# A third tile of state 7 accumulated by VectorE in step 8, and the last image's membrane added by VectorE

## What is computed

```python
def step(h, t):                      # layer 0, over the pixels; 16 states n
    dA = jnp.exp(dt_t[:, :, None] * A)
    dB = dtN_t * B_t
    h = dA * h + dB[:, None, :] * x_t[:, :, None]
    y = jnp.einsum('bdn,bn->bd', h, C_t) + Dskip * x_t
...
def step(v, x_t):                    # layer 1, over the images
    v = v + (x_t - (v - V_RESET)) / TAU
    s = atan_spike(v - V_THRESHOLD)
    v = V_RESET * s_d + v * (1.0 - s_d)
...
x = x + _L0_conv_ref(_gn(x), ...)
x = x + _L1_conv_ref(_gn(x), ...)
```

## Time and profile before

| | |
|---|---|
| median of 3 runs | 4340.82 us (4330.65 to 4343.32) |
| the profiled execution | 4342.65 us |
| its span, first to last instruction | 4340.7 us |
| busy: VectorE, GpSimd, PE, ScalarE | 91%, 89%, 83%, 80% |
| time in the 768 pairs of scans on VectorE | 2730.8 us |
| mean granted TensorE clock | 0.926 of full speed |

### The profile page before, as it was taken

The page is one execution under the profiler, slowest core; times in us unless marked ns, Lnnn a source line. Parts: engine busy times, 40 slices in busy tenths (PEclk is TensorE's granted clock), DMA queues, the critical chain, the costliest instruction groups (busy, mean ns, idle before and its releaser), DMA issues.

```text
span 4340.7 us, 64778 instructions
## 1 busy us (share of the span) xinstructions
PE 3593.2 (83%) x20628; PEld 2275.0 (52%) x20628; DVE 3951.9 (91%) x3833; ACT 3452.2 (80%) x5878; POOL 3847.0 (89%) x2518
## 2 busy tenths in 40 slices
PE   6788888888888888888888888888888888888877
PEld 3455555555555555555555555555555555555554
DVE  3999999999999999999999999999999999999994
ACT  3788887888888888888887888888888888888874
POOL 3999999889998899988998889988899889998993
PEclk8899999999999999999999999999998999999988
DMA  5223323332233223322232223222332233223310
GB/s 132 64 80 96 85 60 92 91 101 62 77 92 101 75 62 100 95 78 71 87 99 75 75 76 99 82 75 75 107 86 64 75 102 101 65 60 100 90 42 22
DMA packets 189296, 355.05 MB, mean 82 GB/s; under 512 B 27416, under 2 KB 164120, under 8 KB 188960
## 3 DMA queue, kind: packets, MB, share of 16 engines
q1 hardware_dynamic: 188960, 350.92, 28.3%
HBM read 289.84 MB, written 61.01 MB: 81 GB/s over the span
## 4 chain that ended last, share of the span: by engine, by line
PE 27%; ACT 23%; DVE 22%; issue 17%; POOL 10%; DMA 0%; DVEq 0%; ACTq 0%; SPq 0%; POOLq 0%
DVE st L1059 17%; PE ht L1197 8%; POOL st L608 8%; ACT decay L736 6%; ACT L933 3%; PE work L1273 3%; PE work L1230 2%; DVE y L1035 2%; ACT dt L809 2%; ACT weighed L765 2%; PE work L1299 2%; PE work L1280 2%; ACT L809 2%; PE work L1170 2%; PE work L1240 2%
## 5 line engine op out<-in xcount | busy, mean ns | idle before, releaser
L1059 DVE TENSOR_TENSOR_SCAN st<-decay,st 128x1024 f32<-128x1024 f32 (+1 forms) x1536 | 2730.8, 1778 | 137.0 <-ACT decay L736 106.7
L608 POOL TENSOR_TENSOR st<-xc,bbc 128x1536 f32<-128x1536 f32 x768 | 2652.8, 3454 | 57.5 <-DMA bbc<-brow 50.9
L736 ACT ACTIVATE decay<-dt,neg_a 128x1024 f32<-128x1024 f32 (+1 forms) x1536 | 1353.7, 899 | 356.2 <-DVE st L1059 349.0
L1197 PE MATMUL ht<-ident,st 128*128 128x128 f32 x9216 | 1326.8, 294 | 291.9 <-DVE st L1059 268.4
L1197 PEld LDWEIGHTS ht<-ident,st 128*128 128x128 f32 x9216 | 1114.5, 151 | 596.3 <-DVE st L1059 448.0
L1035 DVE SCALAR_TENSOR_TENSOR y<-ht,ct,y 128x512 f32<-128x512 f32 x1536 | 1120.3, 729 | 66.1 <-PE ht L1197 64.8
L641 POOL TENSOR_TENSOR y<-y,weighed 128x512 f32<-128x512 f32 x672 | 856.5, 1275 | 278.3 <-ACT weighed L765 276.8
L765 ACT ACTIVATE weighed<-ht,ct 128x512 f32<-128x512 f32 x672 | 459.1, 683 | 230.8 <-PE ht L1197 226.7
L1170 PE MATMUL work<-tri,conv_w 96*32 96x384 f32 x4608 | 433.5, 511 | 11.6 <-DMA tri<-rows_of_xh 4.4
L1235 PE MATMUL work<-xn,win 128*128 128x384 f32 x768 | 329.5, 572 | 94.8 <-DVE volt L1015 58.6
L1230 PE MATMUL work<-xn,win 128*128 128x384 f32 (+1 forms) x768 | 297.5, 511 | 5.8 <-ACT xn L865 3.2
(11 more groups left out here) (114 smaller groups left out, 3368.0 us busy)
## 6 DMA issues: line engine op xcount, KB each, us to landing
bbc<-brow SPq DMA_DIRECT2D x192, 768.0 KB, 6.6
tri<-rows_of_xh SPq DMA_DIRECT2D x576, 200.0 KB, 4.2
rows_of_xh<-xhp SPq DMA_DIRECT2D x160, 200.0 KB, 1.9
out_dram<-ot SPq DMA_DIRECT2D x43, 384.0 KB, 3.8
xin<-in_x_dram SPq DMA_DIRECT2D x42, 384.0 KB, 3.8
rows_of_xh<-xhp SPq DMA_DIRECT2D x32, 250.0 KB, 2.1
st<-in_x_dram SPq DMA_DIRECT2D x6, 384.0 KB, 5.5
out_dram<-y SPq DMA_DIRECT2D x4, 384.0 KB, 2.5
```

What stands on the lines that cost most here:

```text
L608: u = g.tensor_tensor(slot, xc[:, kq % 2, :, :], bbc[:, piece_slot(kq, p), n % PIECE, :].unsqueeze(1).to_broadcast([P, DC, T]), ALU.mult)
L736: a.activation(flat(decay[:, :, :])[:, lo:hi], flat(dt[:, (k + ahead) % 2, :, :])[:, lo:hi], ACT.Exp, scale=neg_a[:, n:n + 1]).then_inc(s_ ...
L1059: v.tensor_tensor_scan(state[:, lo:hi], flat(decay[:, :, :])[:, lo:hi], state[:, lo:hi], 0.0 if h == 0 else state[:, lo - 1:lo], ALU.mult, ...
L1197: last = t.transpose(ht[:, m, c * P:(c + 1) * P], st[:, j, c, m * P:(m + 1) * P], ident[:, :])
```

## The change

One number is added to OWN: state 7. So in step 8 of every slice VectorE does the third tile of state 7 itself, ScalarE does not weigh it, and GpSimd does not add it. TensorE's wait before it overwrites the third tile with state 8 goes from ScalarE's semaphore to that of the accumulation. At the end of the program the identity matmul of each of the 12 blocks is gone, and VectorE adds the membrane in PSUM with a new instruction, for which the comparison waits.

```diff
-OWN = (10, 11,)
+OWN = (7, 10, 11,)
...
+        s_end_v = sem("last_image_charged")
...
+                now = ht[:, j % NHT, 0:T]
                 dve.wait_ge(s_end_l, j + 1)
+                v.tensor_tensor(now, now, volt[:, h, cols], ALU.add).then_inc(s_end_v, 1)
                 need(dve, s_end_t, 2 * (kc - 1))
-                v.scalar_tensor_tensor(out=end_spikes(kc, h), in0=ht[:, j % NHT, 0:T], scalar=fire_at[:, h:h + 1],
+                dve.wait_ge(s_end_v, j + 1)
+                v.scalar_tensor_tensor(out=end_spikes(kc, h), in0=now, scalar=fire_at[:, h:h + 1],
                                        in1=img[:, img_par(B, -1), h, cols], op0=ALU.is_ge,
                                        op1=ALU.add).then_inc(s_end_f, 1)
...
-                t.matmul(ht[:, j % NHT, 0:T], ident[:, :], volt[:, h, kc * T:(kc + 1) * T], start=True, stop=False)
                 for hi in range(CH):
                     last = t.matmul(ht[:, j % NHT, 0:T], w1s[:, hi, h * P:(h + 1) * P],
                                     img[:, img_par(B, -1), hi, kc * T:(kc + 1) * T],
-                                    start=False, stop=hi == CH - 1)
+                                    start=hi == 0, stop=hi == CH - 1)
```

## The result

The changed kernel takes 4302.68 us (median of 6 runs, 4296.64 to 4303.89) against 4340.0 us before (6 runs): ratio 0.9914, 95% interval 0.9903 to 0.9925. That is 37 us less; the forecast was 34 us less, 4307 us. The profiled execution took 4302.32 us, its span is 4300.6 us.

What follows compares the result with a forecast made beforehand. ScalarE, without a pause from step 7 on, was taken to bound two of 16 steps, TensorE the end. Main part -26.8 and end -7.5 make -34.3 us from 4342.65; adjusted to the runs' median, 4307 us, range 4293 to 4326.

Steps and rivals of the forecast that it cites:

- 144 waits as three in each slice: VectorE's scans waiting for ScalarE's decay: 144 waits, 106.7 us, read as three at fixed steps in each of 48 slices.
- -0.58 us a slice: Step 8: ScalarE loses one weighing, so all behind it comes 0.58 us earlier; 47 slices, 27.3 us.
- VectorE's 0.65 us is hidden: Before step 9's first scan: VectorE's added instruction, 0.65 us, fits into its waits and costs nothing there.
- The layer 1 slices by the bank of dt's evacuation: 21 slices, step 9: TensorE's layer 1 block awaits the bank ScalarE's dt evacuation frees; block and step 10's scan 0.58 us earlier.
- The clock term: Layer 1 slices, step 9: blocks starting earlier may meet TensorE's full clock in some; 7 us, only in the low end.
- The moved wait on TensorE and GpSimd's saving cost nothing: Step 8: TensorE's wait for VectorE's new instruction costs nothing; GpSimd's dropped 1.26 us addition buys room, no time: 0.
- The last slice, +0.5 us: The last slice has no ScalarE bound, so VectorE's added instruction costs up to 0.65 us, entered as +0.5.
- The end, -7.5 us: End of the program: twelve identity matmuls gone from TensorE, 7.7 us, with about 0.25 us of VectorE's addition showing.
- rival B: End of the program: TensorE stays at half clock, so the end gives +8 instead of -7.5, 4322 us; chance 0.03.
- C: Main part gains nothing, as ScalarE's later decays wait for VectorE's scans; only the end gains, 4333 us; chance 0.09.
- D: Step 8: third tile transposed too late, ScalarE's gain lost and VectorE's 0.65 us exposed; slower, 4364 us; chance 0.03.
- A: The 21 slices with layer 1 give nothing, as TensorE's clock sets the block's end; 4320 us; chance 0.09.

Runs made afterwards that it cites:

- state 7 alone: The first follow-up run: state 7's third tile moved to VectorE, end of the program as in the kernel before; 4306.38 us against 4337.29, ratio 0.993.

## Why the prediction was right, and where it was off

- *ScalarE bounds steps 7 to 9, though VectorE is the busiest.* Right, and shown: with ScalarE's work put back and everything else changed the main gain is gone, to 0.04 us in slice 0.
- *The 34 us as a sum.* That it came out within 3 us is in part luck. In steps 8 and 9 the 26 slices without layer 1 gave 13.6 us and not 15.1 (slice 5, which gave from -0.3 to 1.2 us, and slice 1 of image 0, which gave none; why was not looked into), the 21 with layer 1 gave 16.9 and not 12.2, and 1.8 us of the trace's 40 lie before the first scan, where nothing was changed.
- *144 waits as three in each slice.* They are not: the scan of step 9 waits for its decay in 47 slices, that of step 10 in 26 and that of step 13 in 38, and the rest stand at steps 3 to 8 and 15. The fixed steps were read from the timelines, so no term rests on it. The 47 at step 9 (36.3 us) are all gone after, and those at step 10 fell from 31.3 to 24.1 us.
- *-0.58 us a slice.* Right to 0.03 us in slices 0, and within the full and the half clock class of the slices with layer 1.
- *VectorE's 0.65 us is hidden.* Right in slices 0 and 4, where leaving it out changes nothing. I gave the scan of step 9 in slice 0 as 0.48 us earlier; it is 5.33 us behind the scan of step 8 and was 5.89, so 0.56, as a scan that does not wait starts 0.08 us inside its predecessor's end (1672.72 + 0.74 against 1673.38). This touches no sum. The same overlap is why VectorE's busy time grew by 33 us and not by the forecast 43: the page counts overlapped time once.
- *The layer 1 slices by the bank of dt's evacuation.* The block does start 0.58 us earlier. That the scan of step 10 comes earlier by the same holds only at a given clock. The clock term, which stood only in the range's low end (7 us), gave some 5 us on top in the changed kernel and 6 with state 7 alone. A second bound, the membrane copy behind ScalarE's decays, was overlooked; it moved by the same 0.58 us, so the sum did not suffer.
- *The moved wait on TensorE and GpSimd's saving cost nothing.* The wait is right: transposes of state 8 end at 1851.39 in the slice shown, 0.44 us before the block starts, as allowed for. GpSimd's 1.26 us bought nothing in steps 8 and 9.
- *The last slice, +0.5 us.* It came out +0.2 us in steps 8 and 9, and shorter by 1.1 us in its other steps, so 0.9 us less in all. Its scan of step 13 waited 0.68 us for GpSimd's input before and does not wait after, and with ScalarE's work kept these steps are shorter by 1.05 us too: in this one slice GpSimd's saved addition does pay. I had counted nothing there.
- *The end, -7.5 us.* -7.6 us by the trace from the first block on. The clock reached full at 4278.3, 3.8 us behind the first block, and rival B fell. The Trainium skill, page "TensorE: Matmul & The Clock Gate", part 1, has activity release the clock, and this stretch agrees: TensorE has no pause in it.
- Rivals C and D fell with the first run; A fell as its slices gained most.

## To carry to other kernels

Ask in each stage which wait ends last, and not which engine is busiest: here 0.65 us put on an engine at 91% and 0.58 us taken from one at 80% made the kernel faster, as in two of sixteen steps the second one was the bound. An engine without a pause over several steps lets go of its work through several doors (a decay, a bank, a copy), and a relief counts at each. Where a stage runs at either of two clocks, compare slices of the same clock, or a few microseconds of luck pass for a mechanism.

## What the runs showed of the hardware that was not expected

TensorE without a pause can stay at half clock. In the trial with repeated dt matmuls it was busy 20.00 of 20.00 us from 2838.5 to 2858.5 at a granted clock of 0.50, with dt matmuls of 40 rows and transposes in turn, and six of those matmuls took 8.05 us. The same form took 1.55 us for two in the changed kernel at full clock (0.78 us each, against 1.34). The Trainium skill's page "TensorE: Matmul & The Clock Gate", part 1, has the clock released by activity; this trace shows a stretch without a pause in which it was not released. Whether the form of those instructions is the reason was not tried by itself.
